# Softmax attention loop: maxima reduced two banks at a time, one ring of banks for scores, sums and shifts, the product of sums on GpSimd

## The reference

```python
q = _rms_norm(x @ wq.T per head); k likewise; both with rope on the last 508 positions
q = q / math.sqrt(HEAD_DIM)
scores = jnp.einsum('bqhd,bkhd->bhqk', q, k)
attn = jax.nn.softmax(scores.astype(jnp.float32), axis=-1)
out = jnp.einsum('bhqk,bkhd->bqhd', attn, v).reshape(b, s, HIDDEN)
return out @ wo.T
```

## Time and profile before

| | us |
|---|---|
| median of three runs | 2090.97 |
| profiled execution | 2091.87 |
| its span, first to last instruction | 2090.1 |
| TensorE busy, whole span | 1788.5 (86%) |
| VectorE busy | 1634.7 (78%) |
| ScalarE busy | 1470.4 (70%) |
| GpSimd busy | 303.9 (15%) |

### The profile page before, as it was taken

How to read it: one execution, slowest core, us unless ns; L and a number is a source line. 1 busy time by engine, 2 the same in 40 slices (tenths; PEclk the granted TensorE clock), 3 DMA queues, 4 the chain that set the end, 5 groups by cost and what they waited for, 6 DMA issues and landing times. The chain is left out here.

```text
span 2090.1 us, 42067 instructions
## 1 busy us (share of the span) xinstructions
PE 1788.5 (86%) x16365; PEld 769.2 (37%) x16365; DVE 1634.7 (78%) x2909; ACT 1470.4 (70%) x2809; POOL 303.9 (15%) x604
## 2 busy tenths in 40 slices
PE   4864879555599999999999999999999999999998
PEld 4544643433386233333233333333233333333334
DVE  3742437654455899999999999999999999999992
ACT  2102547323443588888888888888888888888888
POOL 2371027341030000000000000000000000001211
PEclk9887989566688799999999999999999999999999
DMA  7014111302021001001011010010100101001001
GB/s 244 21 53 115 47 46 52 95 30 60 0 30 52 1 2 17 15 4 17 1 17 17 1 17 5 14 17 2 17 8 11 17 1 17 11 7 22 17 11 51
DMA packets 64293, 61.84 MB, mean 30 GB/s; under 512 B 10752, under 2 KB 52736, under 8 KB 64096
## 3 DMA queue, kind: packets, MB, share of 16 engines
q1 hardware_dynamic: 57952, 46.56, 9.7%
q0 software_dynamic: 6144, 12.60, 2.0%
HBM read 23.21 MB, written 22.94 MB: 22 GB/s over the span
## 5 line engine op out<-in xcount | busy, mean ns | idle before, releaser
L1632 DVE TENSOR_REDUCE at_tops<-bank 128x1 f32<-128x512 f32 x2048 | 1263.9, 683 | 68.4 <-PE bank L1480 49.2
L1603 ACT ACTIVATE experts_then_probs<-bank 128x512 f32<-128x512 f32 x2048 | 1109.6, 598 | 139.9 <-PE bank L1497 113.2
L1480 PE MATMUL bank<-keys,queries 64*128 64x512 bf16 x2048 | 681.0, 389 | 23.6 <-DVE at_tops L1632 19.2
L1497 PE MATMUL bank<-queries,keys 64*128 64x512 bf16 x2048 | 650.1, 383 | 56.2 <-ACT experts_then_probs L1603 56.2
L1511 PE MATMUL bank<-experts_then_probs,values 128*32 128x256 f32 x8192 | 655.0, 391 | 12.2 <-ACT at_sumsT L1621 8.7
L1497 PEld LDWEIGHTS bank<-queries,keys 64*128 64x128 bf16 x2048 | 131.2, 93 | 509.9 <-ACT experts_then_probs L1603 362.5
L1511 PEld LDWEIGHTS bank<-experts_then_probs,values 128*32 128x32 f32 x8192 | 161.7, 108 | 326.5 <-ACT experts_then_probs L1603 193.4
L1480 PEld LDWEIGHTS bank<-keys,queries 64*128 64x128 bf16 x2048 | 169.9, 93 | 115.4 <-DVE at_tops L1632 83.8
L1428 POOL CAST at_shift<-at_neg 128x8 bf16<-128x8 f32 x64 | 14.0, 219 | 1238.3 <-DVE at_neg L1640 1238.3
L669 DVE COPY ep_weights<-WB 128x642 f32 x72 | 35.8, 497 | 91.4 <-DVE ep_slots L680 46.6
L1596 ACT ACTIVATE queries<-bank 3x512 bf16<-3x512 bf16 x128 | 75.4, 589 | 34.4 <-PE bank L1490 31.3
(11 more groups left out here) (252 smaller groups left out, 1588.2 us busy)
## 6 DMA issues: line engine op xcount, KB each, us to landing
queries<-query_parts SPq DMA_DIRECT2D x192, 32.0 KB
keys<-key_parts SPq DMA_DIRECT2D x192, 32.0 KB
sorted_pairs<-zeros SPq DMA_DIRECT2D x16, 288.0 KB, 3.7
ep_slots<-sorted_pairs SPq DMA_DIRECT2D x6, 768.0 KB, 9.2
made_of_pairs<-ep_slots SPq DMA_DIRECT2D x6, 768.0 KB, 4.1
sorted_tokens<-zeros SPq DMA_DIRECT2D x8, 312.0 KB, 3.4
x<-in_L_attn_x_dram SPq DMA_DIRECT2D x4, 512.0 KB, 6.4
experts_then_probs<-in_L_ffn_W_dram SPq DMA_DIRECT2D x1, 2048.0 KB, 9.8
```

The lines of the kernel that those rows point to most:

```text
L1480: nc.tensor.matmul(bank[:, M_BANK + a % R, :], queries[par][rows, at:at + P], keys[par][rows, kb * CHUNK:(kb + 1) * CHUNK], start=True, st ...
L1497: nc.tensor.matmul(bank[:, S_BANK + s % R, :], keys[par][rows, (s // 2) * P:(s // 2 + 1) * P], queries[par][rows, c * CHUNK:(c + 1) * CHUN ...
L1603: nc.scalar.activation(probs[:, s % PR, :], bank[:, S_BANK + s % R, :], ACT.Exp).then_inc(p_ready, 1)
L1632: nc.vector.tensor_reduce(tops[:, m.number % 2, other_half_of(a) * TPC + a // 2 // QC, a // 2 % QC:a // 2 % QC + 1], bank[:, M_BANK + a % ...
```

## The change

- Maxima are made two at a time into two neighbouring banks (a unit), and one reduction of 1024 elements reads both. There are two places of two banks (banks 3 to 6). TensorE waits for a place before the first product of a unit only. 16 reductions a chunk, and the negation reads 8 x 2 columns.
- Scores come in groups of four: two of head 0, then two of head 1 (`head_of(s)` is `s // 2 % 2`). The maxima beside them take the other head.
- A weighing takes one key tile: both heads and both halves of the queries on the four groups of columns, so the sum fills 256 columns of bank 7 instead of 512. Weighings stand behind odd steps.
- Banks 0 to 2 are one ring that runs on over all chunks, for scores, shift transposes and transposed sums together, in the order of a list `turns`.
- Shift transposes stand before score 28, the transposed sums of the chunk before stand before score 12. Two products in place of four, against `sum_columns` (36 columns).
- ScalarE copies the transposed sums to SBUF (`read_sums`). VectorE takes the reciprocal after the negation of a later chunk, and GpSimd makes the product (`normalise_sums`). Buffers `sumsT`, `inv` and `sums_rows` are double.
- Maxima run 20 ahead instead of 24, and 4 scores instead of 8 stand before the loop.
- The constants added to semaphores at the start, and `Step`, are gone.

```diff
-    R = 3
-    S_BANK, M_BANK, O_BANK, T_BANK = 0, 3, 6, 7
-    AHEAD = 24
-    SHIFTS_AFTER = 6
-    EARLY = 4
+    WIDE = 2
+    PER_TILE = QC // WIDE
+    UNITS = 2 * TPC * PER_TILE
+    HALF = CHUNK // 2
+    R = 3
+    MR = 4 // WIDE
+    S_BANK, M_BANK, O_BANK = 0, 3, 7
+    AHEAD = 20
+    FIRST_SCORES = G
+    SUMS_AT, SHIFTS_AT, COPY_AT = 12, 28, 4
...
+        head_of = lambda s: s // 2 % 2
+        keys_of = lambda s: s // G * 2 + s % 2
+        maximum_of = lambda a: (1 - head_of(a), a // (2 * QC), a // G * 2 % QC + a % 2)
+        unit_bank = lambda u: M_BANK + u % MR * WIDE
+        turns = [("shifts", 0, 0)]
+        for n in range(NCHUNKS):
+            for s in range(S):
+                if s == SUMS_AT and n:
+                    turns.append(("sums", n - 1, 0))
+                if s == SHIFTS_AT and n + 1 < NCHUNKS:
+                    turns.append(("shifts", n + 1, 0))
+                turns.append(("score", n, s))
+        turns.append(("sums", NCHUNKS - 1, 0))
+        bank_of = lambda kind, n, s=0: S_BANK + turn_of[kind, n, s] % R
...
+            def normalise_sums(n):
+                pair, c = divmod(n, QC)
+                pool.wait_ge(sums_read, n + 1)
+                pool.wait_ge(inv_ready, n + 1)
+                ...
+                nc.gpsimd.tensor_tensor(to.rearrange("p t (h e) -> p t h e", h=2), of[:, :, :, 0:DK],
+                                        bc(inv[:, n % 2, :]...), ALU.mult).then_inc(attn_out, 1)
...
+            def free_bank(kind, n, s=0):
+                turn = turn_of[kind, n, s]
+                if turn >= R:
+                    before, m, t = turns[turn - R]
+                    if before == "score":
+                        pe.wait_ge(p_ready, m * S + t + 1)
+                    elif before == "shifts":
+                        pe.wait_ge(shift_in, 2 * (m + 1))
+                    else:
+                        pe.wait_ge(sums_read, m + 1)
...
+                u = m * UNITS + a // WIDE
+                if a % WIDE == 0 and u >= MR:
+                    pe.wait_ge(m_out, u - MR + 1)
...
+            def weigh(n, g, half):
+                ...
+                    if n:
+                        pe.wait_ge(sums_out, n)
+                pe.wait_ge(p_ready, n * S + G * g + 3 + half)
+                kt = 2 * g + half
+                for j in range(4):
+                    q, h = divmod(j, 2)
+                    s = G * g + 2 * h + half
+                    mm = nc.tensor.matmul(bank[32 * j:32 * j + 32, O_BANK, 0:HALF], values[pair % 2][:, kt, h, :],
+                                          probs[:, s % PR, q * HALF:(q + 1) * HALF], start=(kt == 0), stop=(kt == NK - 1),
+                                          tile_position=(0, 32 * j), skip_group_check=True)
...
+                for s in range(FIRST_SCORES, S if last else S + FIRST_SCORES):
+                    score(n + s // S, s % S)
+                    if ahead < NCHUNKS * S:
+                        maximum(*divmod(ahead, S))
+                        ahead += 1
+                    if s == SHIFTS_AT - 1 and not last:
+                        shifts(n + 1)
+                    if s == SUMS_AT - 1 and n:
+                        transposed_sums(n - 1)
+                    g = s // G - 1
+                    if s % G == 1 and g:
+                        weigh(n, g, 0)
+                    if s % G == 3:
+                        if g == 0:
+                            weigh(n, g, 0)
+                        weigh(n, g, 1)
...
+            def read_sums(n):
+                act.wait_ge(turned, n + 1)
+                if n >= 2:
+                    act.wait_ge(attn_out, n - 1)
+                nc.scalar.activation(sums_rows[:, n % 2, :], bank[:, bank_of("sums", n), 0:NSUMS], ACT.Copy).then_inc(sums_read, 1)
...
+                for s in range(S):
+                    exponential(n, s)
+                    if s == COPY_AT - 1 and n:
+                        take_sums(n - 1)
+                    if s == SUMS_AT - 1 and n:
+                        read_sums(n - 1)
+                    if s == SHIFTS_AT - 1 and n + 1 < NCHUNKS:
+                        take_shifts(n + 1)
...
+            for m in range(NCHUNKS):
+                for u in range(UNITS):
+                    h, qt, kb = maximum_of(u * WIDE)
+                    at = unit_bank(m * UNITS + u)
+                    dve.wait_ge(m_ready, m * UNITS + u + 1)
+                    nc.vector.tensor_reduce(tops[:, m % 2, h * TPC + qt, kb // WIDE:kb // WIDE + 1],
+                                            bank[:, at:at + WIDE, :].rearrange("p b n -> p (b n)"), X_AXIS, ALU.max).then_inc(m_out, 1)
+                ...
+                nc.vector.tensor_reduce(neg[:, :], tops[:, m % 2], X_AXIS, ALU.max, negate=True).then_inc(neg_ready, 1)
+                if m >= 2:
+                    invert(m - 2)
```

More of the change, by code:

```diff
@@ L1437, in parts @@
+                nc.gpsimd.tensor_tensor(rest[1], rest[0], of(1), ALU.subtract).then_inc(shift_step, 1)
+                pool.wait_ge(shift_step, 4 * m + 4)
                 before_copy()
-                nc.gpsimd.tensor_copy(place(2), rest[1]).then_inc(shift_ready, 1)
-            pool.wait_ge(cleared, 1)
[L1441 to L1456, removed]
@@ new lines, in _ @@
+            pool.wait_ge(cleared, 1)
+            load(0)
+            parts(0)
+            for n in range(NCHUNKS):
+                pair, c = divmod(n, QC)
+                if n + 1 < NCHUNKS:
+                    parts(n + 1)
+                if n:
+                    normalise_sums(n - 1)
+                if c == 0 and pair + 1 < NPAIRS:
+                    if pair:
+                        pool.wait_ge(p_used, n * S // G)
+                    load(pair + 1)
+                if pair >= NPAIRS - 2:
+                    first = (n - (NPAIRS - 2) * QC) * GATHERED
+                    for t in range(first, first + GATHERED):
+                        gather(pool, t)
@@ L1515, in weigh, with transposed_sums @@
                     mm.then_inc(p_used, 1)
-            zero = Step(None, 0, 0)
-            pe.wait_ge(q_loaded[0], 16 * LOADS[0])
-            pe.wait_ge(k_loaded[0], 16 * LOADS[1])
+            def transposed_sums(n):
+                pe.wait_ge(sums_out, n + 1)
+                free_bank("sums", n)
+                out = bank[:, bank_of("sums", n), 0:NSUMS].rearrange("p (q t e) -> p q t e", q=2, t=2)
+                for t in range(2):
+                    mm = nc.tensor.matmul(out[:, :, t, :], sumsT[:, n % 2, t * P:(t + 1) * P],
+                                          k.sum_columns[:, :].rearrange("p (q e) -> p q e", q=2), start=True, stop=True)
+                mm.then_inc(turned, 1)
@@ L1588, in _ @@
-            turns(pe, pair_steps)
+                    shifts(0)
+                if a >= AHEAD - FIRST_SCORES:
+                    score(0, a - (AHEAD - FIRST_SCORES))
+            for n in range(NCHUNKS):
+                last = n == NCHUNKS - 1
+                ahead = (n + 1) * S + AHEAD
+                for s in range(FIRST_SCORES, S if last else S + FIRST_SCORES):
[14 more added lines that the diff above has]
+                        weigh(n, g, 1)
@@ L1590, in _, with take_shifts @@
+            for half in range(2):
+                weigh(n, S // G - 1, half)
+            transposed_sums(n)
         @block.scalar
         def _(act):
-            def take_shifts(m, par, c):
-                act.wait_ge(shiftT_ready, m.at(1, 1))
+            def take_shifts(m):
+                act.wait_ge(shiftT_ready, m + 1)
+                pair, c = divmod(m, QC)
                 for h in range(2):
                     rows = slice(h * HEAD_ROWS + SHIFT, h * HEAD_ROWS + SHIFT + PARTS)
-                    nc.scalar.activation(queries[par][rows, c * CHUNK:(c + 1) * CHUNK],
-                                         bank[rows, T_BANK, 0:CHUNK // 2].bitcast(BF16), ACT.Copy).then_inc(shift_in, 1)
+                    nc.scalar.activation(queries[pair % 2][rows, c * CHUNK:(c + 1) * CHUNK],
+                                         bank[rows, bank_of("shifts", m), 0:HALF].bitcast(BF16), ACT.Copy).then_inc(shift_in, 1)
@@ L1670, in finish @@
+            for n in range(NCHUNKS - 2, NCHUNKS):
+                invert(n)
 def finish(k, w, attn, g_rows, r, out_dram):
```

282 lines of the change are left out of this document (89 added, 193 removed).

## The result

1988.74 us median (1988.13 to 1989.30, 4 runs) against 2090.74: ratio 0.9511, 95% interval 0.9495 to 0.9528, 102 us or 4.9% faster. Forecast 1995, range 1978 to 2041. The profiled execution took 1988.23 us, its span is 1986.1.

What follows compares the result with a forecast made beforehand. TensorE's pace plus its hindrances was taken to set the chunk, 21.46 us falling to 19.98. 62 chunks x 1.48 = 91.8, plus 0.9 at the end and 3 at the start, 95.7 in all: 1995 us, range 1978 to 2041.

Steps and rivals of the forecast that it cites:

- Reduction over two banks: VectorE: 16 reductions of 1024 elements a chunk replace 32, starts 1.12 us apart, ends 1.07 and 1.20.
- Rival B: VectorE: the reduction over two banks saves nothing (1.20 us between starts); 0.75 us a chunk saved, 2041 us; chance 0.10.
- Numbering: Places counted on over all chunks: TensorE's waits of +0.73 us (maxima) and most of +0.85 (scores) go.
- the wait of 1266.23: TensorE in the kernel before: a maximum waits for VectorE, +0.73 us a chunk, put down to how places are numbered.
- TensorE's pace: TensorE: a pair of steps stays at 1.107 us with scores in a new order, ends -0.05 and +0.19.
- rival D: TensorE: two weight loads of 93 ns a pair come bare, 3.0 us a chunk against 1.48 saved, 2181 us; chance 0.07.
- Sums: TensorE: with two products in place of four, the extra for sums falls from 1.10 to 0.65 us a chunk.
- Behind the shift copies: TensorE: scores 30 and 31 wait for ScalarE after its shift copies, +0.15 and +0.39 us a chunk.
- Negation and reciprocal: VectorE: they need 0.30 + 0.20 us a chunk and put its next reduction off; TensorE then waits +0.22.
- The start: Before the loop: 56 reductions become 26 pairs, 4 scores instead of 8 follow; 3 us saved, ends 0 and 6.
- The end: Last stretch, no maxima left: smaller sums and the missing ring wait save about 0.9 us.
- Rival C: Two double places hand over coarsely, so TensorE's pauses starve VectorE: chunk 20.4 us, 1.05 saved, 2022 us; chance 0.12.

Runs made afterwards that it cites:

- half_reduced: The changed kernel with each reduction reading only the first of its two banks, exponent scaled by 0.01: 1966.89 us (a single run), chunk 19.59.
- single: The changed kernel with units of one bank instead of two: four places and 32 reductions of 512 elements a chunk; 1982.56 us, chunk 19.71.
- ring: The kernel before with one part of the change alone, score and maximum places counted on over the chunks: 2059.81 us, chunk 20.94.
- half_shift: The changed kernel with half of ScalarE's shift copies left out, exponent scaled by 0.01: 1962.93 us (a single run), chunk 19.39.
- product: The changed kernel with the product of sums back on VectorE, one reduction after the reciprocal: 1993.42 us, chunk 19.94.
- moved: The changed kernel with the reciprocal moved from behind the negation to ahead of a chunk's eighth reduction: 1982.87 us, chunk 19.70.
- tail: The changed kernel with, in the last chunk alone, scores alternating between row halves and the product of sums on VectorE: 1985.70 us.
- single_tail: The changed kernel with units of one bank, the reciprocal ahead of reduction 14, and last-chunk scores alternating and product on VectorE: 1972.62 us, chunk 19.61.

## Why the prediction was right, step by step

The mechanism was right: TensorE's pace plus its hindrances sets the chunk. Three steps were off: what the numbering is worth for the maxima, the size of several hindrances, and the end.

- *Bound.* Right: half_reduced gives 0.22 us a chunk, where the walk gives VectorE 0.22 and the trace 0.21.
- *Reduction over two banks.* 1.131 for 1.12 (1.115 and 1.13 walked). Rival B is out. The Trainium skill ("Perfetto Trace Analysis", section "Optimizing Scalar/DVE Operations") gives some 125 ns of overhead for a VectorE instruction on PSUM. The trace does not agree: two single ones take 1.196, so merging saved 0.065. (The lower end of 1.07 doesn't follow from its rows: 0.598 less 0.517 is 0.081, not 0.066. No other term uses it.) What I failed to ask is whether the merging earns anything: by single it costs 0.10 a chunk. The gain that stays without it comes from the rest of the change: the numbering (0.52 alone, by ring), the smaller sums (1.10 to 0.56), VectorE's other work, and four banks for maxima where there were three. No run takes the fourth bank away.
- *Numbering.* Right for the scores, wrong for the maxima. I put the wait of 1266.23 down to the numbering. By ring numbering is worth 0.49 at the scores and 0.07 at the maxima, where 0.80 of waiting for VectorE stays. In the kernel after it is 0.21. So most of that hindrance went by something else, the fourth bank or VectorE's shorter list.
- *TensorE's pace.* 1.107 held, rival D is out.
- *Sums.* +0.56 for +0.65. The extra fell by half, so the 0.2 that I kept whole for the switch was too much.
- *Shift transposes.* +0.35 for +0.43. They now stand between a score and its weighing and not between two steps; that this is why is not shown.
- *Behind the shift copies.* +0.63 for +0.54: 0.22 and 0.41 for 0.15 and 0.39. half_shift shows that the copies cause it.
- *Chunk start.* +0.33 for +0.37.
- *Negation and reciprocal.* VectorE's pause was 0.41 for 0.50, TensorE's wait 0.21 for 0.22. That a longer or shorter pause passes to TensorE whole is shown by product and moved.
- *The chunk.* The walk gave 19.92; I took 19.98; it is 19.81. 62 x (1.645 - 1.48) = 10.2 us of the error.
- *The start.* 3 us forecast, 5.3 found. From the first reduction to the first negation it is 18.85 us for 19.26, from there to the second 19.75 for 24.63. The loop itself began 0.45 us earlier, which is chance. Of the 4.9 between the negations 3.8 stay in single (20.82) and none in ring (24.63).
- *The end: wrong.* I had 0.9 us saved and it lost 3.8 (50.8 us from the last negation to the end before, 54.5 after). `finish` begins 33.57 us behind the last negation for 30.45 before. In tail it begins at 29.50, so the 0.9 is there. Over it lie 2.8 of GpSimd's drain behind the product (by product) and 1.2 of scores on the same rows without maxima beside them. The last 0.6 of the 3.8 is `finish` itself and within its scatter. I had costed the product on GpSimd at nothing "since nothing near waits": true in 63 chunks, not in the last.
- *The sum.* The chunks and the start took 12.5 us more than forecast off the time, the end 4.7 less. That the forecast lies within 6 us is partly the luck of two errors that cancel; without the second it would have missed by 11.
- *Rival C, lumps.* Its mechanism is real and its price was too high: VectorE idles 0.93 us a chunk and not 1.8, and single units are 0.10 us a chunk faster, not 0.4. The Trainium skill (same page and section) advises breaking instructions up where an engine that isn't saturated causes gaps on others. The runs agree, though VectorE is busy 94% of the time: single against after (19.71 and 19.81), and single_tail against moved (19.61 and 19.70).

What stays open: how the fall of TensorE's wait for VectorE, from 0.80 in ring to 0.21, splits between the fourth bank and VectorE's shorter list. A kernel with the change but three banks for maxima wasn't tried.

## What to carry to other kernels

When three engines are all near full, walk one period of the in-order engine and list its pauses; a term counts by where it stands, not by its size: the reciprocal cost 0.11 us a chunk in one slot and nothing in another. Count ring places on over the period's end if the period isn't a multiple of the ring. Before merging instructions to save fixed cost, try the same buffers in finer units.

## What the runs showed of the hardware

- A drain of GpSimd at the end of a block took 3.01 us in the trace of after (1961.91 to 1964.92), beside a product of 0.29 us, and the next block's first instructions stand behind it at 1965.17. With that product on VectorE the next block began 2.65 us sooner relative to it.
- Two score products in a row took 0.60 us together on the same half of TensorE's rows and 0.48 on opposite halves, with their weighing 1.10 and 0.98 a pair (the latter at ScalarE's pace). With the other half busy with maxima it makes no difference: 1.107 in both orders.
- A VectorE operation on small operands in SBUF, recorded with 0.20 to 0.22 us, lets the next reduction start 0.12 to 0.13 after its own start; the product from PSUM 0.28, the reciprocal from PSUM 0.35.
- A reduction of two neighbouring banks, 1024 elements, starts its successor after 1.131 us, one of 512 after 0.598: the second bank costs 0.533.
